# A mixer step fewer ahead of the experts, two mixer steps in pieces between expert tiles

## The chip, the cores and the metric

The kernel runs on one core of a Trainium2 chip. The metric is the time of one execution on the device in microseconds, as the median of several runs.

## The reference

The input x has 32 sequences of 256 tokens with 128 features, 8192 tokens in all. Two branches read its layer norm, and the output is x plus both.

```python
xn = layernorm(x)
# mixer
x_proj, z = split(xn @ W_in.T)                    # 256 and 256 features
x_conv = silu(causal_conv(x_proj, 4 taps) + conv_b)
B, C, dt_in = split(x_conv @ W_x.T)               # 16, 16, 256
dt = softplus(dt_in @ W_dt.T + b_dt)
alpha = sigmoid(0.1 * dt)
h = scan(clip(alpha, 0.01, 0.99), (1 - alpha) * sigmoid(mean(B)) * x_conv)
y = (h * sigmoid(mean(C)) + D * x_conv) * silu(z)
mixed = y @ W_out.T
# experts: 8 of them, 128 -> 256 -> 128, each token goes to its best two
hidden = silu(xt @ w1[e]) * (xt @ w3[e])
moe = sum over the two of softmax share * (hidden @ w2[e])
out = x + mixed + moe
```

## The kernel before

**Stages.** The opening normalises the rows, transposes them into `xnT` (16 groups of 512 tokens), computes the expert choices and a slot for every (token, expert) pair. POOL scatters each row to its two slots in DRAM (`moe_in`, line 600; 128 scatters of 128 rows). Meanwhile the mixer handles its 16 groups one after the other in steps. Then the experts work through `MOE_TILES` = 36 tiles: 31 of 512 rows of one expert, 4 whose halves belong to two experts, 1 of 256 rows. The tail finishes the mixer steps that are left, while POOL adds the experts' results, block by block, to the output (14 accumulating DMAs of 512 KB, line 628, in the order of `SUMS`).

**A mixer step.** On PE, step g is `project(g)` (L746, into PC), `gates(g)` (L703), `convolved(g)` (L755 and L759, the input of step g+1, into PA), `gated(g)` (L765, into PB), `spread(g)` (L717, the two gates of the step before, broadcast over the partitions) and `out(g)` (L731, the output product of the step before that). ACT computes softplus in parts (Abs L1133, Exp L1137, Ln L1139, between the table loads L1128 and L1157), the decay (`decay_th` L1110, `decay_al` L1118), the last tap (L1088) and the SiLUs (L1095, L1099, L1103). DVE has the other taps (L1492, three of them), `softplus(g)` (L1473), `turn(g)` (L1482), `add_out(g)` (L1502, adds an output to `xacc`) and `chain(g)`: seven operations counted in `s_ch` (L1386 to L1415), scans among them (L1404), and the product with the gated input (L1424).

`STEPS_A` = 12 steps (0 to 11) run ahead of the experts. Step 11 is the held one: ACT copies its gates from PSUM into `held_g` (L1148), so that PD becomes free for the experts, and DVE does the chain of step 11 between tiles 0, 1 and 2. Step 12 is begun among the tiles: PE's `spread(12)` behind tile 1, the decay on ACT at tiles 3 and 4, DVE's `early_chain` at tiles 4 to 11, and `project(12)` just before the last down product. Steps 12 to 15 are finished in the tail.

**Row scatters.** `follow` (line 575) holds each of the 128 scatters back. From the 39th on, nine go into each mixer step, released by `pace(g, at)`:

```python
def pace(g, at):
    at_chain = {1: 1, 3: 4, 5: 5, 6: 6, 7: 7}
    ...
elif i >= 39:
    pace((i - 39) // 9 + 1, (i - 39) % 9)
```

**An expert tile.** PE: `up(t)` (L861, L862, L865: twelve products of 512 columns in a split of high and low parts, to PA and PB), `transp(t + 1)` (L842, to PD), `down(t - 1)` (L899, sixteen products, to the other half of PD). ACT: rounds the next weights (`round_w`, L1173), `gate(t)` (SiLU of PA, L1202), rounds the next rows (`round_x`, L1196). DVE: low part of weights (L1635) and rows (L1622), `glu` (L1629), the shares and destinations (L1662 to L1681), `scale_y` (L1690, scales a tile's result into one of `OUTS` = 8 buffers). POOL scatters the result of each tile in four scatters (L614), paced by PE's progress. SP loads weights and rows. All engines work in the order in which their instructions are written. On PE tiles 2 to 27 are a hardware loop over pairs (`pe.Fori`), on ACT tiles 11 to 28, on DVE loops of eight tiles; the others are written out.

**Stores.** Blocks of 1024 tokens whose mixer part is complete go to the output by SP (`store_base`, L449 and L451; `STORED` = 6 blocks): four ahead of the experts, the fifth behind the loads of tile 3, the sixth (L491) behind the last expert load. The sums of blocks 0 to 5 are added in the output itself; block 6 is summed in `xacc`, block 7 on PE from rows that SP loads (L497).

## Time and profile before

| | |
|---|---|
| median of 3 runs | 474.4 us (473.97 to 475.49) |
| span of the profiled execution | 553.9 us |
| PE busy | 459.8 us (83%) |
| DVE busy | 394.6 us (71%) |
| POOL busy | 312.4 us (56%) |
| ACT busy | 288.3 us (52%) |
| granted TensorE clock, mean | 0.945 |

The profile is of one execution with the profiler on, whose own time is its span; the runs are made without it. Busy shares are of the span. The profile's lines speak of idle time before an instruction and of what released it; "remote" and "another core or an unknown queue" mean that a semaphore moved at a time for which no instruction's record accounts. A "x4" in a timeline merges four instructions; a matmul of 512 columns in full precision appears as two.

### The profile page before, as it was taken

The page shows a single profiled execution, that of the slowest core. Times are in us where ns is not written, and L with a number is a line of the kernel's source. Part 1 is how long each engine was busy: PE and PEld are TensorE (multiplying, and loading weights), DVE is VectorE, ACT ScalarE, POOL GpSimd, SP SyncE. Part 2 cuts the span into 40 slices and gives each one's busy share as a digit, 9 for nine tenths or more (in the row PEclk, how much of TensorE's full clock was granted, in tenths as well). Part 3 has the DMA queues.
Part 4 walks back from the last instruction along what each step waited for, and adds up shares of the span by engine and source line. Part 5 has one row for each costly group of instructions (what it writes and reads, how often), then busy time and mean ns, then how long its engine had stood idle before and what let it go on. Part 6 is the DMA issues. An engine that isn't in the chain of part 4 may idle for free.

```text
span 553.9 us, 8718 instructions
## 1 busy us (share of the span) xinstructions
PE 459.8 (83%) x2440; PEld 324.4 (59%) x2440; DVE 394.6 (71%) x836; ACT 288.3 (52%) x406; POOL 312.4 (56%) x344
## 2 busy tenths in 40 slices
PE   0987646999999999879979869696987798979876
PEld 0884222445544455448867658585876688745455
DVE  5997551989999999878856675454635465549987
ACT  3772126878888888785533333232423232466880
POOL 4657763767767675711666656565665655663300
PEclk9999777899999999999989999797989898899999
DMA  9921114112121212235556544453543453209992
GB/s 249 283 84 52 54 64 163 50 36 83 49 77 44 82 44 72 78 98 152 164 172 179 168 134 143 120 147 122 156 135 113 126 162 107 71 2 189 243 210 80
DMA packets 48076, 65.91 MB, mean 119 GB/s; under 512 B 8424, under 2 KB 30223, under 8 KB 48048
## 3 DMA queue, kind: packets, MB, share of 16 engines
q1 hardware_dynamic: 36240, 39.56, 25.5%
q0 software_dynamic: 10656, 24.47, 16.1%
q10 hardware_dynamic: 1152, 1.57, 0.9%
q8 instruction: 10, 0.16, 0.1%
q14 instruction: 18, 0.15, 0.1%
HBM read 42.09 MB, written 33.83 MB: 137 GB/s over the span
## 4 chain that ended last, share of the span: by engine, by line
PE 31%; DVE 22%; another core or an unknown queue 18%; issue 16%; ACT 8%; SPq 2%; DMA 1%; DVEq 1%; ACTq 0%
PE PC L746 5%; PE PB L731 4%; PE PD L899 4%; DVE hbuf L1404 3%; PE PA L759 2%; DVE hbuf L1415 2%; DVE gbuf L1289 2%; PE PA L865 2%; PE PA L861 1%; DVE gbuf L1386 1%; DVE xnT L1690 1%; PE PA L862 1%; DVE y L1424 1%; DVE al L1389 1%
## 5 line engine op out<-in xcount | busy, mean ns | idle before, releaser
L614 POOL DMA_INDIRECT moe_out<-xnT,dst_u x142 | 143.1, 1008 | 114.7 <-DVE xnT L1690 51.2
L600 POOL DMA_INDIRECT moe_in<-xn,slot_u x128 | 137.7, 1076 | 65.6 <-issue 41.1
L1202 ACT ACTIVATE xn<-PA 128x1024 f32<-128x1024 f32 (+1 forms) x36 | 36.5, 1015 | 95.1 <-PE PA L865 52.0
L1629 DVE TENSOR_TENSOR xn<-xn,PB 128x1024 f32<-128x1024 f32 (+1 forms) x36 | 43.3, 1204 | 43.1 <-remote 19.0
L899 PE MATMUL PD<-xnT,xn 128*128 128x128 f32 x536 | 68.1, 281 | 6.1 <-DVE xnT L1690 5.7
L899 PEld LDWEIGHTS PD<-xnT,xn 128*128 128x128 f32 x536 | 64.2, 196 | 8.5 <-issue 4.9
L746 PE MATMUL PC<-xc,Wc 128*128 128x512 f32 x128 | 59.9, 612 | 2.8 <-ACT xc L1099 2.8
L759 PE MATMUL PA<-xnT,Wtap 128*128 (+4 forms) x128 | 59.1, 604 | 0.4 <-issue 0.4
L1690 DVE TENSOR_TENSOR xnT<-PD,slot_p 128x512 f32<-128x512 f32 (+1 forms) x36 | 24.5, 681 | 39.6 <-remote 35.1
L861 PE MATMUL PA<-xhi,whi 128*128 128x512 f32 x62 | 29.4, 474 | 26.6 <-ACT xhi L1196 16.7
L1196 ACT ACTIVATE xhi<-PD 128x512 fp32r<-128x512 f32 (+1 forms) x36 | 21.2, 589 | 49.7 <-remote 32.6
L759 PEld LDWEIGHTS PA<-xnT,Wtap 128*128 128x128 f32 x128 | 24.9, 195 | 32.8 <-issue 32.8
L746 PEld LDWEIGHTS PC<-xc,Wc 128*128 128x128 f32 x128 | 24.0, 197 | 28.1 <-issue 24.8
L765 PE MATMUL PB<-xnT,WinT 128*128 (+1 forms) x64 | 31.7, 620 | 7.9 <-ACT nbdt L1009 7.7
L1492 DVE SCALAR_TENSOR_TENSOR acc<-PA,cw,acc 128x510 f32<-128x510 f32 (+2 forms) x48 | 35.6, 741 | 3.4 <-ACT acc L1088 2.4
L1404 DVE TENSOR_TENSOR_SCAN hbuf<-al,gbuf 128x512 f32<-128x512 f32 x30 | 35.0, 1208 | 0.1
L1133 ACT ACTIVATE ebuf<-PC,bdt 128x512 f32<-128x512 f32 x32 | 20.3, 684 | 24.4 <-PE PC L746 15.3
L1622 DVE TENSOR_TENSOR xlo<-PD,xhi 128x512 fp32r<-128x512 f32 (+1 forms) x36 | 24.4, 678 | 11.7 <-ACT xhi L1196 10.3
L731 PE MATMUL PB<-WoT,y 128*128 128x128 f32 x192 | 25.9, 292 | 5.8 <-DVE y L1424 4.9
L861 PEld LDWEIGHTS PA<-xhi,whi 128*128 128x128 f32 x62 | 12.8, 207 | 30.3 <-issue 28.7
L1110 ACT ACTIVATE th<-ebuf,bdt 128x512 f32<-128x512 f32 x32 | 21.3, 714 | 14.7 <-issue 12.8
L731 PEld LDWEIGHTS PB<-WoT,y 128*128 128x128 f32 x192 | 23.9, 202 | 8.5 <-DVE y L1424 6.6
(244 smaller groups left out, 963.2 us busy)
## 6 DMA issues: line engine op xcount, KB each, us to landing
xnT<-moe_w SPq DMA_DIRECT2D x36, 256.0 KB
xn<-moe_in SPq DMA_DIRECT2D x31, 266.0 KB
out_dram<-moe_out POOLq DMA_DIRECT2D x12, 512.0 KB, 11.8
xnT<-moe_w SPq DMA_DIRECT2D x36, 128.0 KB
out_dram<-xacc SPq DMA_DIRECT2D x7, 512.0 KB, 10.0
moe_out<-xnT,dst_u POOLq DMA_INDIRECT x142
moe_in<-zrow SPq DMA_DIRECT2D x8, 266.0 KB
moe_w<-in_L_ffn_w_dram SPq DMA_DIRECT2D x2, 1024.0 KB
```

The source lines that it names most:

```text
L600: gp.indirect_dma_start(xs_dram, bass.IndirectOffsetOnAxis(ap=slot_u[:, k, j:j + 1], axis=0), xn_row[:, j, :], None).then_inc(s_scat, 16)
L614: gp.indirect_dma_start(yt_dram, bass.IndirectOffsetOnAxis(ap=dst_u[:, t, j:j + 1], axis=0), yo[t % OUTS][:, j, :], None, bounds_check=PAI ...
L731: last = pe.matmul(PB[:, at + j * D:at + (j + 1) * D], y[:, k, j * P:(j + 1) * P], WoT[:, k, :], start=(k == 0), stop=(k == 1))
L746: last = pe.matmul(PC[:, c_ * GROUP:(c_ + 1) * GROUP], Wc[:, k, c_ * P:(c_ + 1) * P], xc[:, slot, k, :], start=(k == 0), stop=(k == 1))
L759: last = pe.matmul(both[:, :, j:SEQ], Wtap[:, TAPS - 1 - j, :], src[:, :, 0:SEQ - j], start=(j == 0), stop=(j == TAPS - 1))
L765: last = pe.matmul(PB[:, c_ * GROUP:(c_ + 1) * GROUP], WinT[:, INNER + c_ * P:INNER + (c_ + 1) * P], source(g), start=True, stop=True)
L861: pe.matmul(o, whi[:, b, at], xhi[:, b, :], start=True, stop=False)
L899: last = pe.matmul(PD[:, 512 + j * D:512 + (j + 1) * D], hid[b][:, k * SLOTS + j * P:k * SLOTS + (j + 1) * P], (w2x[t - FULL] if mixed and ...
L1202: act.activation(halves(sil, t), halves(PA[:, :], t), ACT.Silu).then_inc(s_sil, 1)
L1404: last = ve.tensor_tensor_scan(hbuf[:, c_, :], al[:, c_, :], gbuf[:, c_, :], 0.0, ALU.mult, ALU.add)
L1492: ve.scalar_tensor_tensor(a_v, p_v[:, :, 0:SEQ - j], cw[:, 1, TAPS - 1 - j:TAPS - j], a_v, ALU.mult, ALU.add).then_inc(s_taps if j == TAPS ...
L1629: ve.tensor_tensor(halves(hid[b], t), halves(sil, t), halves(PB[:, :], t), ALU.mult).then_inc(s_hid, 1)
```

## The change

Eleven steps (0 to 10) run ahead, step 10 is the held one. Steps 11 and 12 (`INNER_STEPS` = 2) are done in twelve pieces each, at the tiles in `INNER_AT` for step 11 and 15 tiles (`CYCLE`) later for step 12; step 13 (`STEPS_B`) gets its first five pieces at tiles 31 to 35. On PE the pieces are 1 `spread`, 2 gates, 3 `out`, 4 and 5 the halves of `project`, 8 and 9 the halves of `convolved`, 10 `gated`. All of them use PC in place of PA, PB and PD. ACT copies the spread gates to `held_g` at piece 1 (`hold_among`) for each of these steps, and has the table loads with exponential and logarithm in piece 6. DVE has `chain` cut into eight (`chain_among`) with `turn`, `add_out`, `softplus` and the taps. All loops over tiles on PE, ACT and DVE are written out. In the tail, steps 13 to 15 are left. From the 39th scatter on, ten go into a step; the tenth waits for the step's softplus. SP's fifth `store_base` moves behind its loop over tiles.

```diff
-STEPS_A = 12
+STEPS_A = 11
+INNER_STEPS = 2
+STEPS_B = STEPS_A + INNER_STEPS
+CYCLE = 30 // INNER_STEPS
+INNER_AT = (1, 2, 4, 5, 7, 8, 10, 11, 13, 14, 16, 17)
...
-STORED = STEPS_A // 2
+STORED = 6
...
+        def pieces(t):
+            found = [(STEPS_A + n, at + 1) for n in range(INNER_STEPS) for at in range(len(INNER_AT))
+                     if n * CYCLE + INNER_AT[at] == t]
+            last = t - INNER_STEPS * CYCLE
+            return found + [(STEPS_B, last)] if last >= 1 else found
...
-            sp.wait_ge(s_xp, 12)
-            sp.wait_ge(s_z, 12)
+            sp.wait_ge(s_xp, 11)
+            sp.wait_ge(s_z, 11)
...
-            store_base(STORED - 2)
-
             with sp.Fori(0, (FULL - 4) // 2) as i:
...
+            store_base(STORED - 2)
...
-                else:
-                    gp.wait_ge(s_y2, g)
+                elif at == 8:
+                    gp.wait_ge(s_y2, g)
+                else:
+                    gp.wait_ge(s_dt, g + 1)
...
-                    pace((i - 39) // 9 + 1, (i - 39) % 9)
+                    pace((i - 39) // 10 + 1, (i - 39) % 10)
...
+            def mixer_piece(g, at):
+                if at == 1:
+                    spread(g)
+                elif at == 2:
+                    gates_among(g)
+                elif at == 3:
+                    out(g, g % SLOT3, True)
+                elif at == 4:
+                    project_among(g, 1)
+                elif at == 5:
+                    project_among(g, 0)
+                elif at == 8 and g < STEPS_B:
+                    convolved_among(g, 0)
+                elif at == 9 and g < STEPS_B:
+                    convolved_among(g, 1)
+                elif at == 10 and g < STEPS_B:
+                    gated_among(g)
...
-            spread(STEPS_A)
-            with pe.Fori(0, (FULL - 4) // 2) as i:
-                up(i * 2 + 2, 0, False)
-                transp(i * 2 + 3, i + 1, 1, False)
-                down(i * 2 + 1, i, 1, False)
-                up(i * 2 + 3, 1, False)
-                transp(i * 2 + 4, i + 2, 0, False)
-                down(i * 2 + 2, i + 1, 0, False)
-            for t in range(2 + (FULL - 4) // 2 * 2, MOE_TILES):
+            for piece in pieces(1):
+                mixer_piece(*piece)
+            for t in range(2, MOE_TILES):
...
                 down(t - 1, (t - 1) // 2, (t - 1) % 2, False)
-            project(STEPS_A, STEPS_A % SLOT3, True)
+                for piece in pieces(t):
+                    mixer_piece(*piece)
...
+            def mixer_piece(g, at):
+                if at == 1:
+                    hold_among(g)
+                    decay_th(g)
+                elif at == 2:
+                    decay_al(g)
+                elif at == 4:
+                    row_tanh(g)
+                elif at == 5:
+                    abs_among(g)
+                elif at == 6 and g < STEPS_B:
+                    act.preload_act_table_set("natural_log_exp_and_others")
+                    logs_among(g)
+                    act.preload_act_table_set("silu_and_others")
...
-            turns = (FULL - 1 - opening) // 2
-            with act.Fori(0, turns) as i:
-                tile_step(i * 2 + opening, i + opening // 2, 1, True)
-                tile_step(i * 2 + (opening + 1), i + (opening + 1) // 2, 0, True)
-            for t in range(opening + 2 * turns, MOE_TILES):
+            for t in range(3, MOE_TILES):
                 tile_step(t, t // 2, t % 2, t + 1 < MOE_TILES)
+                for piece in pieces(t):
+                    mixer_piece(*piece)
...
+            for t in range(3, MOE_TILES):
                 static_step_v(t)
+                for piece in pieces(t):
+                    mixer_piece(*piece)
...
+            g = STEPS_B
+            chain_among(g, 3)
+            chain_among(g, 4)
+            softplus(g)
+            for n in (5, 6, 7):
+                chain_among(g, n)
+            for g in range(STEPS_B, GROUPS - 1):
```

## Rows read from the trace of the kernel before

**Rows 1.** Page: the span.

```profile
span 553.9 us, 8718 instructions
```

**Rows 2.** Page, part 4: shares of the chain that ended last, by engine.

```profile
PE 31%; DVE 22%; another core or an unknown queue 18%; issue 16%; ACT 8%; SPq 2%; DMA 1%; DVEq 1%; ACTq 0%
```

**Rows 3.** Busy time by stage: opening, mixer steps, expert tiles, tail.

```profile
core 0: us, PE busy (x) PEld busy (x) DVE busy (x) ACT busy (x) POOL busy (x), PEclk, DMA share, GB/s
0.00:96.30 96.30, 60.98 (x300) 41.89 (x301) 62.05 (x276) 42.09 (x87) 56.67 (x98) 0.90 0.45 137
96.30:238.20 141.90, 133.98 (x621) 71.35 (x621) 130.22 (x169) 113.03 (x140) 99.96 (x90) 0.98 0.20 63
238.20:482.80 244.60, 205.97 (x1220) 175.19 (x1219) 147.22 (x320) 91.39 (x129) 134.22 (x133) 0.93 0.47 138
482.80:553.90 71.10, 58.85 (x304) 35.94 (x302) 55.13 (x72) 41.79 (x53) 21.55 (x23) 0.98 0.67 142
```

**Rows 4.** The same view: tiles 3 to 28, tiles 29 to 34, tiles 21 and 22.

```profile
261.90:432.60 170.70, 143.28 (x834) 121.72 (x833) 102.15 (x221) 57.17 (x81) 103.17 (x103) 0.94 0.50 146
432.60:477.40 44.80, 37.06 (x242) 33.95 (x241) 23.85 (x56) 15.61 (x23) 25.96 (x27) 0.89 0.44 125
383.90:393.90 10.00, 10.00 (x65) 8.86 (x64) 5.87 (x14) 3.42 (x6) 5.92 (x6) 1.00 0.34 101
```

**Rows 5.** Waits in the expert tiles: us in total, times, longest.

```profile
ACT xhi L1196 <- remote: 32.6, 8, 6.1
```

**Rows 6.** Timeline of ACT in the opening.

```profile
59.20 0.60 ACT L1006 ACTIVATE Wc<-PB 128x512 f32<-128x512 f32 x1 [7.36 <-issue]
...
69.00 1.02 ACT L1082 ACTIVATE sz<-PB 128x1024 f32<-128x1024 f32 x1 [7.83 <-remote]
```

**Rows 7.** Timeline of PE: first projections of two mixer steps, eight steps apart.

```profile
111.33 0.59 PE L746 MATMUL PC<-xc,Wc 128*128 128x512 f32 x1
...
222.54 0.59 PE L746 MATMUL PC<-xc,Wc 128*128 128x512 f32 x1
```

**Rows 8.** Timeline of PE: one mixer step.

```profile
195.37 3.60 PE L746 MATMUL PC<-xc,Wc 128*128 128x512 f32 x8
198.81 1.88 PE L765 MATMUL PB<-xnT,WinT 128*128 x4
200.62 0.64 PE L703 MATMUL PD<-xc,WgS 128*32 128x128 f32 x16
...
202.15 3.58 PE L759 MATMUL PA<-xnT,Wtap 128*128 x8
205.57 1.05 PE L717 MATMUL PD<-ident,tg 128*128 128x128 f32 x8
207.09 2.05 PE L731 MATMUL PB<-WoT,y 128*128 128x128 f32 x16 [0.47 <-DVE y L1424]
```

**Rows 9.** Timeline of POOL: two of the last row scatters.

```profile
232.50 0.96 POOL L600 DMA_INDIRECT moe_in<-xn,slot_u  x1 [0.30 <-issue]
...
235.47 1.62 POOL L600 DMA_INDIRECT moe_in<-xn,slot_u  x1 [0.30 <-issue]
```

**Rows 10.** Timeline of ACT ahead of the first expert tile.

```profile
242.15 1.28 ACT L1128 ACT_TABLE_LOAD   x1
243.45 1.27 ACT L1133 ACTIVATE ebuf<-PC,bdt 128x512 f32<-128x512 f32 x2
244.75 1.06 ACT L1137 ACTIVATE ebuf<-ebuf 128x1024 f32<-128x1024 f32 x1
```

**Rows 11.** Timeline of PE in the tail: projections of steps 14 and 15.

```profile
514.29 3.70 PE L746 MATMUL PC<-xc,Wc 128*128 128x512 f32 x8 [1.35 <-ACT xc L1099]
...
527.03 2.41 PE L746 MATMUL PC<-xc,Wc 128*128 128x512 f32 x5 [1.41 <-ACT xc L1099]
```

**Rows 12.** Timeline of POOL: the last scatter of expert rows.

```profile
493.90 0.98 POOL L614 DMA_INDIRECT moe_out<-xnT,dst_u  x1 [0.30 <-issue]
```

**Rows 13.** Busy time while the sums run.

```profile
496.80:539.60 42.80, 38.54 (x192) 22.57 (x190) 39.31 (x50) 33.29 (x42) 12.70 (x14) 0.96 1.01 206
```

More of the change, by code:

```diff
@@ L832, in _, with gates_among @@
             pe.sem_inc(s_out, 1)
-            mixer(pe, mix, 0, STEPS_A)
+            mixer(pe, mix, 0, STEPS_A - 1)
+            mixer(pe, mix, STEPS_A - 1, STEPS_A)
+            def gates_among(g):
+                slot = g % SLOT3
+                pe.wait_ge(s_xc, g + 1)
+                pe.wait_ge(s_hold, holds(g))
+                for k in range(HALVES):
+                    for j in range(STRIPS):
+                        last = pe.matmul(PC[j * STRIP:(j + 1) * STRIP, GROUP:GROUP + P], WgS[:, k, :],
+                                         xc[:, slot, k, j * P:(j + 1) * P], start=(k == 0), stop=(k == 1))
+                last.then_inc(s_g, 1)
@@ new lines, in project_among @@
+            def project_among(g, c_):
+                slot = g % SLOT3
+                if c_ == 1:
+                    pe.wait_ge(s_lt, g + 1)
+                else:
+                    pe.wait_ge(s_add, g)
+                for k in range(HALVES):
+                    last = pe.matmul(PC[:, c_ * GROUP:(c_ + 1) * GROUP], Wc[:, k, c_ * P:(c_ + 1) * P],
+                                     xc[:, slot, k, :], start=(k == 0), stop=(k == 1))
+                if c_ == 0:
+                    last.then_inc(s_u, 1)
@@ new lines, in convolved_among @@
+            def convolved_among(g, part):
+                both = PC[:, 0:GROUP].rearrange("p (s l) -> p s l", s=SPG)
+                src = source(g).rearrange("p (s l) -> p s l", s=SPG)
+                if part == 0:
+                    pe.wait_ge(s_dt, g + 1)
+                    pe.matmul(PC[:, GROUP:2 * GROUP], WinT[:, P:2 * P], source(g), start=True, stop=True).then_inc(s_xr, 1)
+                for j in range(2 * part, 2 * part + 2):
+                    last = pe.matmul(both[:, :, j:SEQ], Wtap[:, TAPS - 1 - j, :], src[:, :, 0:SEQ - j],
+                                     start=(j == 0), stop=(j == TAPS - 1))
+                if part == 1:
+                    last.then_inc(s_xp, 1)
@@ new lines, in gated_among @@
+            def gated_among(g):
+                pe.wait_ge(s_c0, g + 2)
+                pe.wait_ge(s_taps, g + 2)
+                for c_ in range(HALVES):
+                    last = pe.matmul(PC[:, c_ * GROUP:(c_ + 1) * GROUP],
+                                     WinT[:, INNER + c_ * P:INNER + (c_ + 1) * P], source(g), start=True, stop=True)
+                last.then_inc(s_z, 1)
+            def mixer_piece(g, at):
[15 more added lines that the diff above has]
+                    gated_among(g)
@@ L934, in _ @@
             pe.wait_ge(s_hid, MOE_TILES)
-            gates(STEPS_A, STEPS_A % SLOT3, True)
-            for g in range(STEPS_A, GROUPS - 1):
+            for g in range(STEPS_B, GROUPS - 1):
                 pe.wait_ge(s_taps, g + 1)
@@ L1212, in tile_step, with hold_among, abs_among @@
                     round_x(t + 1, 1 - b)
+            def hold_among(g):
+                act.wait_ge(s_gb, g)
+                act.wait_ge(s_ch, (g - 2) * CHAIN + C_USED)
+                act.activation(held_g[:, :, :], PC[:, :].rearrange("p (n l) -> p n l", n=2), ACT.Copy).then_inc(s_hold, 1)
+            def abs_among(g):
+                act.wait_ge(s_u, g + 1)
+                act.wait_ge(s_th, g)
+                for c_ in range(HALVES):
+                    last = act.activation(ebuf[:, c_, :], PC[:, c_ * GROUP:(c_ + 1) * GROUP], ACT.Abs,
+                                          bias=bdt[:, c_:c_ + 1])
+                last.then_inc(s_abs, 1)
@@ L1231, in _ @@
             round_x(2, 0)
+            for piece in pieces(1):
+                mixer_piece(*piece)
             round_w(3, 1, 1, False)
```

182 lines of the change are left out of this document (108 added, 74 removed).

## The prediction

> **What bounds the kernel now.** The page's first line gives a span of 553.9 us [rows 1]; the unprofiled runs have a median of 474.4 us, 79.5 us less. The chain of waits shows what kind of time differs: 18% of the span (about 100 us) is put down to no engine [rows 2]. The view by stage cuts the span into four [rows 3]: the opening 96.3 us, eleven mixer steps and a bit 141.9 us (PE busy 134.0), the expert tiles 244.6 us, the tail 71.1 us. In the expert tiles, two neighbours can run at 5.0 us each with PE busy all the time, yet 32 tiles take 170.7 + 44.8 = 215.5 us, 6.73 each, 55.5 us over 32 x 5.0 [rows 4]. The excess sits in single holes: ACT waits eight times, up to 6.1 us, for a transpose whose record had long ended [rows 5]. ACT shows the same holes in the opening, 7.36 and 7.83 us [rows 6]. I read them as mostly the profile's own cost, since the runs are 79.5 us shorter and nothing else has such holes. The sum is therefore a difference, made in the profile's durations and added to 474.4; by itself it would put the next span near 551.
>
> How much of the 55.5 is real decides the sign. If the opening owes only its two longest ACT waits [rows 6], 15.2 of the 79.5 us, the other 64 are more than all holes of the tiles: no slack, 5.0 us per tile. If it owes twice that and the tail 4, the tiles owe 45 and keep 10 us in which PE really waits. Call this slack s, between 0 and 10.
>
> **One step fewer ahead.** From the projection of one step to that of the eighth after it: 222.54 - 111.33 = 111.2, so 13.9 us a step [rows 7]. Removed: **-13.9**. Everything that waits on the step count moves with it: SP's first weight loads wait for eleven convolutions instead of twelve, the held gates for step 10.
>
> **Row scatters.** 128 scatters, 39 before the paced ones; 89 at nine a step end in step 10, at ten a step in step 9. The last one runs at 235.47 [rows 9], just ahead of the first tile, and would stand in the same place relative to the shorter front. POOL needs 0.96 + 0.30 = 1.26 us for one [rows 9], so ten take 12.6 of 13.9: it fits with 1.3 us left. No row shows ten in a step. Its price lies between 0 and, if each of the eight added ones held a step up whole, 8 x 1.26 = 10 us; a gain has no source, as their number is the same. I take **0**, because nine already run beside 13.9 us steps with 2.6 us idle.
>
> **PE work put among the tiles.** One step on PE, start to start [rows 8]: projection 3.44 (195.37 to 198.81), gated input 1.81, gates and convolution 4.95 (200.62 to 205.57), spread 1.05, output 2.05 less the 0.1 in which it overlaps the next; together 13.2. Steps 11 and 12 go in whole, step 13 without convolution (4.95 less 0.64 for the gates) and gated input: 3 x 13.2 - 4.3 - 1.8 = 33.5. Spread and projection of step 12 stood there already: 1.05 + 3.44. Net **+29.0** us of PE among 36 tiles. Where PE is busy without a hole all of it is on the path; the slack covers s.
>
> **DVE and ACT among the tiles.** DVE works 102.15 / 26 = 3.9 us in a tile [rows 4]; a piece adds 0.7 to 2.3. With 5.0 us and PE's own piece beside it, it fits but for the tiles of two experts, where it comes level. ACT is the tight one: piece 6 puts table load, exponential, logarithm and table load in one run, 1.28 + 1.06 + 1.06 + 1.28 = 4.7 us [rows 10], in a tile with no PE piece to stretch it (tiles 8 and 23). With the tile's own 57.17 / 26 = 2.2 us [rows 4] ACT needs 6.9 where PE needs 5.0. PE can go on for about 0.4 us of that: 1.5 us lost, twice. **+3**. From below 0 (a late gate covered), from above 10 (every piece of ACT and DVE a hole of half a microsecond, some twenty of them).
>
> The row shows the next activation 0.02 us behind the table load, 243.45 against 242.15 + 1.28 [rows 10]. The Trainium skill, "ScalarE: Activation LUTs", section "What ACT_TABLE_LOAD costs", counts a drain of 1.38 us with each switch; four switches would then cost 5.5 us more, and the sum would end at 476.9 instead of 471.4. The trace shows no such drain, so I leave it out.
>
> **Other moves.** PE, ACT and DVE no longer loop over tiles. I cost that at 0: tiles 22 and 23 stand 5.0 us apart across a turn of PE's loop, and unlooped tiles (29 to 34, 44.8 / 6 = 7.5) have as many holes as looped ones (170.7 / 26 = 6.6) [rows 4]. ACT copies the spread gates to held_g, about 1.0 us a step, beside PE's next tile. SP moves one 512 KB store behind its loop and one ahead of the last scatter; nothing waits for either but the sums.
>
> **Tail.** One step fewer: projections of 14 and 15 stand 527.03 - 514.29 = 12.7 us apart [rows 11]. The first step is no faster: before, PE reaches project(13) behind two outputs; after, DVE reaches the taps of step 13 behind both scans, softplus and three chain pieces, by my count of its rows at the same point, 16 us behind the last up product. **-12.6**, if the DMAs allow it (a rival below). Bounds: -6 by that rival, -15 if both outputs' 3.8 us come off too.
>
> **Sum.** -13.9 + 29.0 - s + 3 - 12.6 = +5.5 - s. For s I take 8.5, nearer to 10 than to 0: POOL issues four scatters a tile at 0.98 + 0.30 us [rows 12], 5.1 us, so that tiles can't average 5.0, and 36 x 0.1 = 4 us of slack are there by this alone; and the wait of 7.36 us in the opening [rows 6] is a hole of the same kind as the others, which speaks for the larger share there. So -3.0: **471.4 us**. Break-even is s = 5.5. With s from 10 to 4 this case runs from 469.9 to 475.9; below s = 4 it is the first rival.
>
> **Rivals.** *PE has no slack* (slower). Place: PE's in-order queue in the tiles. s = 0 and 6 us of stalls instead of 3 (a piece waits for DVE's scan or ACT's copy, and the next up product queues behind it): -13.9 + 29.0 + 6 - 12.6 = +8.5, **482.9**. It decides as soon as s falls under what the pieces stall plus 2.5. For it: 10.0 of 10.0 us busy in tiles 21 and 22 [rows 4]. Against: POOL's 5.1 us a tile.
>
> *The holes are real* (faster). If PE idles in the runs as in the profile, even by a third of the 55.5, pieces disappear in it: s = 20, **459.9**. For it: the chain of the profile. Against: the 79.5 us must come from somewhere, and the holes are the only place. The Trainium skill, "Runtime: NRT & Kernel Launch", section "Instruction fetch mechanics", says a taken branch can force a fetch before going on; 13 turns of PE's loop would then go away and the time would end in this rival's place. The trace speaks against it: unlooped tiles have the holes too.
>
> *The sums set the end* (no change or slower). The last scatter runs at 493.90 [rows 12], the end is 60.0 us later; a step less makes it 47.4. The sums hold the DMAs from 496.8 to 539.6, at a share of 1.01 and 206 GB/s [rows 13], and can't start before the last scatter: 45.7 us, less 2.5 for the 0.5 MB store that is now done earlier. That leaves 4 us for last rows, loads and stores, which now share the DMAs with the sums. If they queue behind them half of the tail's gain goes: -6 instead of -12.6, **478.0**.
>
> *It doesn't do what it says*: the tenth scatter waits for the softplus of its step, and if POOL then falls behind, the first rows are late; up to +10, inside the slower cases.
>
> **How the numbers follow.** A measurement tells 0.3%, 1.4 us, from no change. Forecast case 0.38 (faster 0.26, same 0.10, slower 0.02); holes real 0.19 (faster); no slack 0.30 (slower 0.28, same 0.02); sums 0.13 (faster 0.01, same 0.03, slower 0.09). Together faster 0.46, same 0.15, slower 0.39. The likeliest case's own range is 467 to 476. The whole range takes in the fast rival and the slow one with 2 us beyond: 458 to 485.
>
> **What would show it.** Right: first tile's transposes 14 us earlier; last transposes and last scatter about 20 us later relative to them, at unchanged or slightly higher cost per hole; tile pairs without pieces at 10.0 us, with pieces longer by exactly PE's piece; from last up product to the end 12 to 13 us less. Wrong: the tiles' stretch grows by clearly more than 28 or less than 12; ACT's piece 6 followed by a PE hole over 2 us; step length ahead of the experts over 14.5; DMA share at 1.0 up to the last store.

## The result, and the profile after

The changed kernel takes **496.0 us** (median of 4 runs, 495.7 to 497.3) beside 474.4 for the kernel before (474.0 to 475.5): ratio 1.047, interval 1.045 to 1.050 (the two medians alone give 1.046). It is slower by 21.6 us. Every ratio here leaves out single runs that took over 1.5% more than the fastest run of the same kernel. The prediction was 471.4 us, and its range (458 to 485) doesn't hold the result.

The page of the changed kernel, its first line, the line of PE, DVE, ACT and POOL, and the chain by engine, as [rows 1, 2]:

```profile
span 493.9 us, 8449 instructions
...
PE 434.3 (88%) x2440; PEld 310.6 (63%) x2440; DVE 394.2 (80%) x836; ACT 290.6 (59%) x409; POOL 316.3 (64%) x344
...
PE 47%; DVE 29%; issue 11%; ACT 6%; POOL 3%; DMA 2%; ACTq 0%; DVEq 0%; SPq 0%
```

The span is 2.1 us under the runs' median, and the 18% of "another core or an unknown queue" of [rows 2] is gone. So the trace of before that the prediction read and this trace don't show the same situation: its span was 79.5 us over its kernel's median. Which of the two is odd was settled by the experiments. They ran on four chips. On two of them the kernel before has medians of 473 to 475 us and shows no holes, on the other two it takes 545 to 561 us unprofiled as well; the two chips that were used in two series came out alike both times. The trace of [rows 1 to 13] looks like the second kind in its span and its holes; the two times of the result are of the first. I call them the 474 us chips and the 554 us chips. A profile of the kernel before on a 474 us chip (run i1) is therefore the one to hold against the profile after. Busy time by stage, cut at the transposes of the first and of the 36th expert tile; first the kernel before, on a 474 us chip:

```profile
core 0: us, PE busy (x) PEld busy (x) DVE busy (x) ACT busy (x) POOL busy (x), PEclk, DMA share, GB/s
0.00:217.60 217.60, 194.05 (x948) 113.32 (x948) 196.44 (x452) 162.54 (x236) 151.15 (x188) 0.98 0.35 105
217.60:393.40 175.80, 173.78 (x1145) 154.90 (x1146) 141.00 (x305) 84.06 (x117) 124.53 (x122) 1.00 0.63 184
393.40:472.10 78.70, 63.67 (x349) 40.35 (x347) 57.60 (x79) 42.65 (x54) 35.82 (x35) 0.94 0.62 137
238.10:363.00 124.90, 124.76 (x801) 110.66 (x800) 99.17 (x212) 56.50 (x78) 95.98 (x95) 1.00 0.65 192
```

then the changed kernel:

```profile
0.00:214.30 214.30, 179.79 (x887) 105.76 (x887) 184.84 (x437) 152.10 (x222) 150.49 (x188) 0.97 0.35 106
214.30:424.20 209.90, 204.84 (x1300) 173.40 (x1301) 157.42 (x329) 106.93 (x147) 137.84 (x129) 0.99 0.55 157
424.20:493.90 69.70, 49.63 (x256) 31.41 (x254) 51.97 (x70) 31.62 (x40) 28.01 (x28) 0.89 0.69 148
```

Front 3.3 us shorter, 35 tiles 34.1 longer, tail 9.0 shorter: -3.3 + 34.1 - 9.0 = +21.8, the difference of the spans (493.9 - 472.1). In the tiles PE was busy 173.78 of 175.80 us before (124.76 of 124.90 in the middle ones) and is busy 204.84 of 209.90 after: 31.1 us more work and 3.0 us more idle time. Some 1.5 us of that work is the first tile, which holds no piece: PE is busy for 5.55 us in it, at a granted clock of 0.58, where it was for 4.04 us at 1.00.

**The front, after.** POOL's last two row scatters, SP's loads of the first rows, PE's first transposes:

```profile
207.63 0.96 POOL L617 DMA_INDIRECT moe_in<-xn,slot_u  x1 [0.30 <-issue]
208.90 0.96 POOL L617 DMA_INDIRECT moe_in<-xn,slot_u  x1 [0.30 <-issue]
```

```profile
211.38 0.85 SPq L482 DMA_DIRECT2D xn<-moe_in  x2
```

```profile
214.28 1.09 PE L923 MATMUL PD<-ident,xn 128*128 128x128 f32 x4 [11.60 <-DMA xn<-moe_in]
```

PE has finished its eleventh step at 202.7 us, where it finished the twelfth at 217.2 before, and waits 11.6 us for rows; they can be loaded only behind the 128th scatter. From 205.3 to 214.2 us PE and ACT do nothing. In the kernel before, the last scatter starts at 210.48 and PE comes to the tiles at 217.62, 0.44 us of wait behind DVE:

```profile
210.48 0.96 POOL L600 DMA_INDIRECT moe_in<-xn,slot_u  x1 [0.30 <-issue]
```

```profile
217.62 0.66 PE L842 MATMUL PD<-ident,xn 128*128 128x128 f32 x4 [0.44 <-DVE lgt L1482]
```

**The tail, after.** POOL's last expert scatter and first sum, and VectorE's last addition (the span ends at 493.94):

```profile
442.98 0.98 POOL L631 DMA_INDIRECT moe_out<-xnT,dst_u  x1 [0.30 <-issue]
445.88 1.27 POOL L645 DMA_DIRECT2D xacc<-moe_out  x1 [1.92 <-issue]
```

```profile
485.65 0.42 DVE L1915 TENSOR_TENSOR xacc<-PB,xacc 128x256 f32<-128x256 f32 x1 [0.47 <-PE PB L1059]
```

The same of the kernel before on a 474 us chip (its span ends at 472.10):

```profile
421.01 0.98 POOL L614 DMA_INDIRECT moe_out<-xnT,dst_u  x1 [0.30 <-issue]
423.90 1.50 POOL L628 DMA_DIRECT2D xacc<-moe_out  x1 [1.91 <-issue]
```

```profile
463.74 0.42 DVE L1773 TENSOR_TENSOR xacc<-PB,xacc 128x256 f32<-128x256 f32 x1 [0.47 <-PE PB L983]
```

The end stands 48.1 us behind the first sum after, 48.2 before, and 7.9 us behind the last addition in both. In the kernel before, POOL issues the 142 scatters of expert rows from 231.72 to 421.01 us with a single pause of over 0.4 us (0.56 us): they are a chain as unbroken as PE's, only later. In the changed kernel the same chain has 26 such pauses, 25.7 us in all, in which it waits for the slower tiles. In the trace that the prediction read, the last addition stood 2.3 us before the end, and the tail looked as if VectorE and PE set it.

### The profile page after: what moved, and what is told of

Read it like the earlier page. It is cut to its first block, busy times and chain, and to the rows that moved or that the text cites. A ratio compares the mean times of both kernels' runs of the same rounds, so it can differ in the third digit from the quotient of the medians.

```text
span 493.9 us, 8449 instructions
## 1 busy us (share of the span) xinstructions
PE 434.3 (88%) x2440; PEld 310.6 (63%) x2440; DVE 394.2 (80%) x836; ACT 290.6 (59%) x409; POOL 316.3 (64%) x344
## 4 chain that ended last, share of the span: by engine, by line
PE 47%; DVE 29%; issue 11%; ACT 6%; POOL 3%; DMA 2%; ACTq 0%; DVEq 0%; SPq 0%
PE PD L980 10%; DVE hbuf L1529 4%; PE PB L753 4%; DVE hbuf L1540 3%; POOL moe_in L617 3%; PE PD L923 3%; PE PA L946 3%; PE PB L942 2%; PE PB L943 2%; PE PB L946 2%; PE PA L942 2%; DVE gbuf L1511 2%; DVE gbuf L1414 2%; PE PA L943 2%; DVE acc L1618 2%
## 5 line engine op out<-in xcount | busy, mean ns | idle before, releaser
L631 POOL DMA_INDIRECT moe_out<-xnT,dst_u x142 | 153.6, 1082 | 80.5 <-issue 33.8
L617 POOL DMA_INDIRECT moe_in<-xn,slot_u x128 | 131.6, 1028 | 44.6 <-issue 40.6
L766 PE MATMUL PC<-xc,Wc 128*128 128x512 f32 x104 | 49.8, 624 | 5.8 <-ACT xc L1175 5.8
L779 PE MATMUL PA<-xnT,Wtap 128*128 (+4 forms) x112 | 51.6, 604 | 0.0
L1761 DVE TENSOR_TENSOR wlo<-xnT,whi 128x512 fp32r<-128x512 f32 x36 | 24.7, 685 | 15.3 <-ACT whi L1249 15.1
L1618 DVE SCALAR_TENSOR_TENSOR acc<-PA,cw,acc 128x510 f32<-128x510 f32 (+2 forms) x42 | 31.0, 739 | 1.2 <-ACT acc L1164 0.9
L923 PE MATMUL PD<-ident,xn 128*128 128x128 f32 x142 | 21.8, 276 | 11.6 <-DMA xn<-moe_in 11.6
L1186 ACT ACTIVATE th<-ebuf,bdt 128x512 f32<-128x512 f32 x32 | 21.3, 713 | 13.2 <-DVE ebuf L1598 13.2
L923 PEld LDWEIGHTS PD<-ident,xn 128*128 128x128 f32 x142 | 17.7, 142 | 15.9 <-issue 11.8
L785 PE MATMUL PB<-xnT,WinT 128*128 128x512 f32 (+1 forms) x56 | 26.5, 596 | 1.2 <-ACT bdt L1086 1.0
L1598 DVE SCALAR_TENSOR_TENSOR ebuf<-PC,nbdt,ebuf 128x512 f32<-128x512 f32 x32 | 22.4, 740 | 3.2 <-ACT ebuf L1215 2.0
```

Of the source, the lines that this page charges most:

```text
L617: gp.indirect_dma_start(xs_dram, bass.IndirectOffsetOnAxis(ap=slot_u[:, k, j:j + 1], axis=0), xn_row[:, j, :], None).then_inc(s_scat, 16)
L631: gp.indirect_dma_start(yt_dram, bass.IndirectOffsetOnAxis(ap=dst_u[:, t, j:j + 1], axis=0), yo[t % OUTS][:, j, :], None, bounds_check=PAI ...
L766: last = pe.matmul(PC[:, c_ * GROUP:(c_ + 1) * GROUP], Wc[:, k, c_ * P:(c_ + 1) * P], xc[:, slot, k, :], start=(k == 0), stop=(k == 1))
L779: last = pe.matmul(both[:, :, j:SEQ], Wtap[:, TAPS - 1 - j, :], src[:, :, 0:SEQ - j], start=(j == 0), stop=(j == TAPS - 1))
L785: last = pe.matmul(PB[:, c_ * GROUP:(c_ + 1) * GROUP], WinT[:, INNER + c_ * P:INNER + (c_ + 1) * P], source(g), start=True, stop=True)
L923: last = pe.transpose(PD[:, j * P:(j + 1) * P], xs[b][:, j, 0:D], ident[:, :])
```

## Experiments on the 554 us chips

The first three series ran on chips on which the kernel before takes 551 to 560 us.

**The kernel before again**, twice for a profile (e0, f0): 550.9 and 560.7 us, beside medians of 554.2 and 560.2 for other runs of it.

> The kernel before, unchanged, profiled once more. The changed kernel's profile has a span (493.9) close to its runs (496.0), the one of before did not (553.9 against 474.4). If the holes were an accident of that one profiled execution, this span is near 472 and the expert tiles stand 5.2 to 5.4 us apart; if they belong to the looped kernel under the profiler, it is again near 554 and the holes are back.

> The kernel before, unchanged, for a profile beside the other three on whatever chip this is. Where its runs take 474, I expect a span near 472, no holes, expert tiles 5.2 to 5.4 us apart and an opening some 20 us shorter than in the trace of 553.9. Where they take 554, the same picture as in that trace.

The 35 tiles take 224.0 us in e0 and 232.6 in f0, against 232.7 in the prediction's trace, and the unprofiled time is just as long as the profiled one. The holes are no cost of the profiler, though the prediction had read them so. They go with the chip, or with something around it that no run separates from it. Busy time in the tiles of the kernel before, in f0:

```profile
248.60:481.10 232.50, 195.53 (x1144) 166.32 (x1145) 139.73 (x305) 83.04 (x117) 132.18 (x130) 0.93 0.49 141
```

**The changed kernel again** (f1): 549.3 us, ratio 0.983 (0.974 to 0.993).

> The changed kernel, unchanged, beside the kernel before on one chip. Where the kernel before takes 474: 496 again, 4.7% slower. Where it takes 554 (a chip on which engines stall while POOL's scatters run): theory A, ten scatters a step bring the stalls up, 570 to 590; rival, the holes among the tiles swallow the pieces, 535 to 550.

The change that costs 4.7% on a 474 us chip gains 1.7% here, in the rival's range. The same view of it:

```profile
242.00:472.30 230.30, 212.28 (x1301) 174.46 (x1302) 157.40 (x331) 107.93 (x150) 134.65 (x129) 0.99 0.49 143
```

PE is busy for 16.8 us more in 2.2 us less time: most of the pieces lie in the holes. The pieces need 31.1 us on a 474 us chip, and the clock accounts for the difference of 14.3. The tiles of the kernel before keep PE busy for 195.53 us here, at a granted clock of 0.93 (173.78 at 1.00 on a 474 us chip), those of the changed kernel for 212.28 at 0.99 (204.84 at 0.99). That the filled holes are what keeps the clock up is my reading of these four rows; it was not tried alone.

**Ten row scatters in a step of the kernel before** (e1, f2):

```diff
-                else:
-                    gp.wait_ge(s_y2, g)
+                elif at == 8:
+                    gp.wait_ge(s_y2, g)
+                else:
+                    gp.wait_ge(s_dt, g + 1)
...
-                    pace((i - 39) // 9 + 1, (i - 39) % 9)
+                    pace((i - 39) // 10 + 1, (i - 39) % 10)
```

> The kernel before with ten row scatters a step instead of nine, the tenth behind the softplus; nothing else. Theory A (POOL's scatters are a chain of their own; twelve steps leave it room): no change, 473 to 476, last scatter 5 to 12 us earlier than with nine. Rival (a tenth scatter slows each step): 8 steps longer by up to 1.3 us each, 478 to 484.

> The kernel before with ten scatters a step. On a chip without the stalls: no change (within 2 us of the kernel before), because POOL only finishes earlier. With the stalls: 2.7% slower as measured once already (567 against 554).

Ratios 1.027 (1.014 to 1.041) and 1.023 (1.013 to 1.034): slower here, by 12 to 15 us, which neither the first expectation nor its rival had, since both were made for a 474 us chip.

**Row scatters not paced at all in the changed kernel** (e2; from the 40th on `pace` is left out):

> The changed kernel with the scatters from the 39th on not paced at all. Theory A (the front of the changed kernel waits some 9 us for the last scatter, which paced scatters reach at 208.9 us; unpaced ones end near 200): first tile's transposes at 205 to 207 instead of 214.3, time 487 to 490. Rival (the pace is what keeps the scatters off the steps): steps longer, first tile no earlier, time 495 or more.

621.7 us, ratio 1.130. Busy time of two stretches while the scatters run one behind another:

```profile
100.00:120.00 20.00, 16.83 (x86) 8.43 (x84) 14.35 (x20) 11.25 (x14) 15.43 (x16) 1.00 0.16 52
140.00:160.00 20.00, 2.56 (x11) 2.17 (x12) 3.50 (x6) 0.21 (x1) 15.42 (x16) 0.50 0.16 55
```

POOL works as before, and in the second stretch the others nearly stand still, at a DMA share of 0.16. The last scatter starts at 213.8 us, 21 earlier than in f1, and still PE reaches the first tile only at 323.0 (242.0 in f1): the loss is in the steps and not in the scatters. I can't say what the engines wait for. It goes with the kind of chip: on the 474 us chips POOL issues its scatters without a pause too, as i1 to i3 below show, and the steps keep their 13.4 us.

**Twelve steps ahead, one among the tiles, nine scatters** (e3, f3), and **eleven ahead, one among the tiles, ten scatters** (g1):

```diff
-STEPS_A = 11
-INNER_STEPS = 2
+STEPS_A = 12        (11 in g1)
+INNER_STEPS = 1
...
-                    pace((i - 39) // 10 + 1, (i - 39) % 10)
+                    pace((i - 39) // 9 + 1, (i - 39) % 9)        (not in g1)
```

> The changed kernel with twelve steps ahead and one among the tiles (STEPS_A = 12, INNER_STEPS = 1) and nine scatters a step: only the tail's step is moved. Theory A (11 us of the loss are the scatters at the end of a shorter front, the rest is that PE has no slack among the tiles): front as before, one step of PE work less among the tiles, 478 to 484. Rival (the loss is all in the pieces): 485 to 490. If tiles had slack for one step: 464 to 472.

> Twelve steps ahead, one among the tiles, nine scatters a step. On a chip without the stalls, theory A (some 10 us of the 21.6 are the wait for scatters ahead of the first tile, the rest is PE work among tiles without slack): 478 to 484. Rival (the pieces cost it all): 485 to 490. With the stalls: 547 as measured already.

> Eleven steps ahead, one among the tiles, ten scatters a step (STEPS_A = 11, INNER_STEPS = 1): only the front's step is moved, the tail keeps four. On a chip where the kernel before takes 474: the front gives 14 back less 11 of waiting for scatters, one step and five pieces (15.8 us of PE beyond what stood there) go among the tiles, so 480 to 488 by the theory that the tiles have little slack; under 474 if the loss were in the tail. Where it takes 555: 548 to 560, near the changed kernel, if stalls swallow pieces.

Ratios 0.9925 (0.987 to 0.998), 0.984 (0.972 to 0.996) and 1.015 (1.008 to 1.022); the first two are the same kernel in two series. On such a chip a step moved from the tail to the tiles gains, and one moved there from the front doesn't.

## Experiments on the 474 us chips

**A profile of the kernel before** (i1, 473.9 us):

> The kernel before, unchanged, for a profile on a chip on which it takes 474 us. Both theories: no stretch in which all engines stand still among the tiles, steps ahead 13.4 us apart, first expert tile's transposes at 217.8 as in the kernel with twelve steps ahead and one among the tiles. Theory 1 (no slack): its 35 tiles take 180 us (5.0 each and five longer ones), and the time from the 36th tile's transposes to the end is 74 to 76. Theory 2 (the tiles had slack, and the tail is what grew): tiles of 190 and a tail of 64. Where it takes 554: the profile shows holes again.

No holes; tiles 175.8 us, tail 78.7. Theory 1's numbers were off by 4 (tiles) and 3 (tail), theory 2's by 14 and 15. The rows stand above.

**The same two variants of the split** (h2, h3):

> Twelve steps ahead, one among the tiles (13 in all before the tail's last), nine row scatters a step: against the kernel before, one step leaves the tail and goes into the tiles. If the tiles have no slack and the tail is held by its DMAs, 474 + 14.5 - 3 = 486 (ratio 1.024) on a chip where the kernel before takes 474; if the tail gives all of its 12.6 us, 476. Where the kernel before takes 554: 0.984 to 0.993, as in two earlier runs.

> Eleven steps ahead with ten row scatters each, one step among the tiles, the tail as before: one step leaves the front. If the scatters' own time bounds the front (10 x 1.27 us of 13.4 a step) the front gives 3 of its 13.9 us and the tiles take 14.5: 474 + 11.5 = 485 (ratio 1.024) where the kernel before takes 474; if the front gives all of it, 475. Where the kernel before takes 554: 1.015, as in an earlier run.

487.6 us (ratio 1.029, 1.027 to 1.032) and 489.6 us (1.034, 1.032 to 1.037). Busy time in the tiles and tail, of h2, then of h3:

```profile
217.80:412.50 194.70, 190.22 (x1238) 164.39 (x1239) 146.11 (x314) 96.28 (x133) 133.24 (x127) 1.00 0.58 168
412.50:485.80 73.30, 49.82 (x256) 31.54 (x254) 51.94 (x70) 31.64 (x40) 30.85 (x30) 0.87 0.66 143
```

```profile
214.00:409.20 195.20, 191.26 (x1239) 165.93 (x1240) 144.75 (x312) 95.48 (x132) 133.58 (x127) 0.99 0.58 168
409.20:487.30 78.10, 62.96 (x318) 38.61 (x316) 65.75 (x87) 42.80 (x54) 30.47 (x30) 0.93 0.62 134
```

The first moved step costs 18.9 to 19.4 us among the tiles (194.7 and 195.2 against 175.8), the second 14.7 (209.9 against 195.2). The first brings five pieces of the next step with it: of its 18.9 us in h2, 16.4 are work of PE (190.22 against 173.78) and 2.5 idle time. A step fewer ahead gives 3.3 to 3.8 us (217.6 or 217.8 to 214.0 or 214.3). A step fewer in the tail gives 5.4 (78.7 to 73.3, i1 to h2) or 8.4 (78.1 to 69.7, h3 to the changed kernel). The expectations had 14.5 for the tiles in both, 4.4 to 4.9 us too little, so both kernels came out slower than expected. Neither a shorter front nor a shorter tail pays what a step among the tiles costs; the split of the kernel before is the best of the four on such a chip.

The tail of h3 shows a second path. Its last expert scatter stands 21.3 us behind the 36th tile's transposes, 6.3 less than in i1, yet its tail is only 0.6 us shorter. Its last addition ends 75.9 us behind the same transposes (70.8 in i1) and 2.2 us before the end: with four steps left the mixer sets the end there. The changed kernel has one step less, its last addition comes 61.9 us behind the 36th tile's transposes instead of 75.9, and the sums set the end again.

**Thin pieces** (h1): the pieces' matmuls stream 8 columns, which leaves out most of the mixer's values of three steps. (The convolution's stream 4, and `spread` is as it was.)

```diff
...
-                    last = pe.matmul(PC[:, c_ * GROUP:(c_ + 1) * GROUP], Wc[:, k, c_ * P:(c_ + 1) * P],
-                                     xc[:, slot, k, :], start=(k == 0), stop=(k == 1))
+                    last = pe.matmul(PC[:, c_ * GROUP:c_ * GROUP + 8], Wc[:, k, c_ * P:(c_ + 1) * P],
+                                     xc[:, slot, k, 0:8], start=(k == 0), stop=(k == 1))
...
```

> The changed kernel in which the matmuls of the pieces that follow expert tiles stream 8 columns where they streamed 128 to 512 (the same number of matmuls, waits and signals; the mixer's values of steps 11 to 13 are left out thereby). Theory 1 (TensorE sets the tiles' pace, no slack): on a chip where the kernel before takes 474 us it takes some 20 us less than the changed kernel's 496, about 475, and tiles with a piece of TensorE start 5.3 us apart where they started 6.7. Theory 2 (the pieces on ScalarE and VectorE set it): within 5 us of 496. On a chip where the kernel before takes 554 us, theory 3 (there each tile waits for something that is no engine's work, and the pieces lie under these waits): at most 5 us less than the changed kernel (549 in an earlier run, 0.983 of the kernel before), against 20 less, 0.947, by theory 1.

480.1 us, 15.9 under the changed kernel; the tiles take 195.6 us, 14.3 less, and PE is busy in them for 190.15, 14.7 less. Most tiles with a piece of PE stand 5.4 us apart where they stood 6.7. Time and PE's work fall together: PE sets the tiles' pace, and ACT's and DVE's pieces, all still there, don't, but for the two tiles behind ACT's piece 6 (below). That it fell by 16 and not by 20 is due to how little a narrow matmul saves; the two groups of PE in the tiles of h1:

```profile
L754 PE MATMUL PC<-WoT,y 128*128 128x8 f32 x48 | 5.6, 251 | 0.0
...
L875 PE MATMUL PC<-xc,Wc 128*128 128x8 f32 x16 | 2.0, 236 | 0.0
```

The first number is the busy time of the group in us, in which overlapping matmuls count once, the second the mean of one in ns. In the changed kernel the same two groups are 5.8 us (275 ns each, 128 columns) and 7.5 us (593 ns, 512 columns): 8 columns save nothing against 128, and three quarters against 512.

**Ten scatters in the kernel before** (i2) and **eleven in the changed kernel** (i3; `// 11` and `% 11`, the eleventh waits for nothing):

> The kernel before with ten row scatters in each step ahead in place of nine, nothing else. Theory 1 (GpSimd's own time bounds the front only where eleven steps are to cover it): the last of twelve steps ends after the scatters either way, ratio 0.998 to 1.003. Theory 2 (a tenth scatter disturbs each step): steps of 13.4 grow to 14 or more, 12 x 0.6 = 7 us, ratio 1.015. Where the kernel before takes 554: 1.023 to 1.027 as in two earlier runs.

> The changed kernel with eleven row scatters paced into a step in place of ten (the eleventh waits for nothing). 11 x 1.27 = 14.0 us is more than a step's 13.4, so GpSimd is never idle from the first step on: 89 scatters from 84.6 on end at 198 instead of 208.9. Theory 1 (the scatters' own time holds the first tile back): its transposes start 5.4 us behind the last scatter, at 203 to 206 in place of 214.3, and the time is 8 to 11 us under the changed kernel's 496, 485 to 488. Theory 2 (unpaced scatters slow the other engines' steps): steps grow, the time is 496 or more. Where the kernel before takes 554: theory 2's outcome.

i2: 473.7 us, ratio 0.9989 (0.997 to 1.000): on this kind of chip the tenth scatter costs nothing. i3: 496.6 us, as the changed kernel; theory 1's 485 to 488 is a miss, and theory 2's time is right for the wrong reason, since the steps keep their 13.4 us. The scatters' times say why. In the kernel before, nine a step:

```profile
88.19 0.96 POOL L600 DMA_INDIRECT moe_in<-xn,slot_u  x1 [0.30 <-issue]
...
180.89 1.13 POOL L600 DMA_INDIRECT moe_in<-xn,slot_u  x1 [0.30 <-issue]
182.33 0.96 POOL L600 DMA_INDIRECT moe_in<-xn,slot_u  x1 [0.31 <-issue]
```

These are the 40th, 109th and 110th: 70 scatters in 94.1 us, 1.344 us each and not 1.26, because some of them take 1.13 to 1.30 us instead of 0.96, and with no more than 0.30 us between them. PE takes 94.1 us for seven steps (90.25 to 184.39). POOL already issues ten in a step without a pause, with a pacing of nine, ten or eleven alike, since it starts behind its schedule. The chain is in fact unbroken from its first scatter on, which starts at 36.7 to 36.9 us in these kernels: up to the 112th no pause is over 0.32 us. Ahead of the 114th POOL pauses for 3.1 to 3.7 us, for which the view names no releaser; in i1 it also waits 1.0 us ahead of the 113th. The last scatter starts at 210.5, 209.9, 208.9 and 210.1 us in i1, i2, the changed kernel and i3.

Some three of the ten in a step are long, 27 of the 89 from the 40th on in i1 (one of them takes 1.46 us), and each of these runs beside one of VectorE's operations whose data all lie in SBUF (L1386 and L1389, L1404, L1415 and L1424), such as the first row beside the second:

```profile
176.77 1.30 POOL L600 DMA_INDIRECT moe_in<-xn,slot_u  x1 [0.30 <-issue]
```

```profile
176.08 2.33 DVE L1404 TENSOR_TENSOR_SCAN hbuf<-al,gbuf 128x512 f32<-128x512 f32 x2
```

The Trainium skill, "SBUF — State Buffer", section "SBUF: two separate sides", says that GpSimd can't write its descriptors while some of VectorE's operations hold the port that both share. By that rule each long scatter would be a short wait for this port. The trace agrees, though not simply because the two overlap: 42 of the 62 short ones overlap such an operation at some time too. What tells the two kinds apart is one moment, which I took from the trace itself, 0.15 us behind the scatter's start. Such an operation is running then in all 27 long ones and in none of the 62 short ones of i1, and in i2 in 26 of 26 and none of 63. The added length grows with what is left of that operation: 0.17 us where it ends 0.30 us behind the scatter's start, 0.31 where it ends 0.44 behind it, 0.33 for 0.52. Still, no run took such an operation away, so the cause is argued and not shown.

**Ten fills of an unused buffer between the last scatters** (two ahead of each from the 117th to the 121st), in the changed kernel (j1) and in the kernel before (j2):

```diff
+                        if j * TOP_K + k in (116, 117, 118, 119, 120):
+                            gp.wait_ge(s_fill, 16 * EXPERTS)
+                            for n in range(2):
+                                gp.wait_ge(s_zrow, 1 + 2 * (j * TOP_K + k - 116) + n)
+                                gp.memset(zrow[:, :, :], 0.0).then_inc(s_zrow, 1)
```

> The changed kernel with ten fills of a 128 x 532 buffer (0.56 us each in the profile of the kernel before, 0.6 to 0.7 with their waits) put on GpSimd between the 117th and the 121st row scatter; nobody reads the buffer any more. Theory 1 (GpSimd's chain of 128 scatters sets when the tiles begin): the last scatter starts 6 to 7 us later, at 215 to 216, the first tile's transposes at 220 to 221, and the time is the changed kernel's 496 and 6 to 7: 502 to 503 (ratio 1.060). Theory 2 (the steps or a wait set it, and the scatters have room): 496 to 498. Where the kernel before takes 554: no statement, the changed kernel is 0.983 there.

> The same ten fills in the kernel before. Theory 1: its last scatter starts at 210.5, and 5.4 us behind it is 215.9, while its twelve steps let the tiles begin at 217.6, so it has 1.7 us of room: the tiles begin 4.3 to 5.3 us later and the time is 479 (ratio 1.009 to 1.011). Theory 2 (twelve steps cover the scatters with a whole step's room): ratio 1.000 to 1.002.

j1: 503.1 us, ratio 1.059 (1.055 to 1.063), 7 us over the changed kernel, as theory 1 said (6.5 in the front, and 0.6 in a first tile of 6.85 us instead of 6.28). The last scatter and PE's first transposes in j1:

```profile
215.46 0.96 POOL L622 DMA_INDIRECT moe_in<-xn,slot_u  x1 [0.30 <-issue]
```

```profile
220.81 1.09 PE L928 MATMUL PD<-ident,xn 128*128 128x128 f32 x4 [17.40 <-DMA xn<-moe_in]
```

Both are 6.5 us later than in the changed kernel: in its front POOL's chain of 128 scatters has no room at all. j2: 480.5 us, ratio 1.013 (1.009 to 1.016), 6.0 us against the 4.3 to 5.3 expected. Its front grows by 3.8 us, so the kernel before has under 2 us of room; and its tiles grow by 1.8 (399.0 less 221.4 against 175.8), all of it in the first one (7.08 us instead of 5.17), though not one instruction was added to them. The granted clock shows it. The first tiles in j2, behind 5.2 us in which PE stood still, and the same stretch of i1:

```profile
221.40:241.90 20.50, 19.01 (x97) 15.97 (x98) 15.18 (x32) 10.36 (x15) 3.80 (x4) 0.82 0.48 134
```

```profile
217.60:238.10 20.50, 18.62 (x105) 14.95 (x106) 18.16 (x38) 12.10 (x17) 5.16 (x5) 1.00 0.50 141
```

A share of 0.82 of the 2.4 GHz, an average of both levels, against 1.00; in the same 20.5 us PE finished 97 instructions instead of 105.

**Fewer sums** (i4): six of the fourteen sums in the changed kernel's tail are cut to an eighth (64 of 512 KB; the expectation calls it a quarter), so most rows of the second choice are left out of the stored blocks.

```diff
+                if k < STORED and c:
+                    gp.dma_start(dst[:, 0:1], yt_b[:, k, c, 0:1], accum_op=ALU.add).then_inc(s_got[k], 16)
+                    continue
```

> The changed kernel with six of its fourteen sums in the tail cut to a quarter of their 512 KB (the second choice's rows of the six stored blocks are left out for three quarters of the tokens in them). Theory 1 (the DMAs set the end, 7.8 us behind VectorE's last add): the last store follows the last add by 2 to 3 us, 5 us less in all: 491. Theory 2 (the mixer's last steps set the end): under 1 us less.

490.2 us, 5.8 under the changed kernel. The size of the six, from the issues of DMAs in this run, and the last addition, which is where it was; the span ends at 488.32, 2.3 us behind it instead of 7.9:

```profile
out_dram<-moe_out POOLq DMA_DIRECT2D x6, 64.0 KB, 9.5
```

```profile
485.62 0.42 DVE L1918 TENSOR_TENSOR xacc<-PB,xacc 128x256 f32<-128x256 f32 x1 [0.47 <-PE PB L1062]
```

In the changed kernel the DMAs set the end, by 5.6 us. In the kernel before the end stands as far behind the last addition (7.9 us), but its sums were not cut.

## Why the prediction was wrong, point by point

**The reading of the holes was the root.** The step "I read them as mostly the profile's own cost" fails: on a 554 us chip the unprofiled runs take as long as the profile with the holes (550.9 to 560.7 us). From there the prediction mixed two situations, a trace of one kind of chip and a median of the other, and had to estimate every slack from the difference of 79.5 us.

**Slack s, taken as 8.5: it was 0.** On a 474 us chip PE is busy 124.76 of 124.90 us in the middle tiles, and 99% of all of them. The argument that POOL's 5.1 us a tile would make PE wait fails too: the tiles stand 5.0 us apart and POOL falls behind them instead, its last expert scatter starting 27.6 us after the 36th tile's transposes. That the chosen 8.5 alone gave the forecast its sign is shown by the sum: with s = 0 the sum was +5.5.

**One step fewer ahead, -13.9: it gave -3.3.** The step itself is right (13.4 us on this chip, and PE has finished its steps 14.5 us earlier, at 202.7 instead of 217.2), but "the last one would stand in the same place relative to the shorter front" fails. The scatters are a chain of their own, which ends at 209 to 210.5 us whatever the number of steps; j1 shows that it has no room. The term "row scatters: 0" rested on 1.26 us apiece and on "1.3 us left" in a step; the scatters take 1.344, ten of them a whole step, and the bounds looked at what a scatter does to a step and not at what 128 of them need (172 to 174 us from the first to the last). The rival of the late tenth scatter gave up to +10 for this; its place was right, its mechanism (the wait for softplus) was not: in the changed kernel no scatter up to the 113th waits over 0.32 us for anything.

**PE pieces, +29.0: +31.1 measured.** Some 1.5 us of it are the first tile at a lower clock (0.58), which follows PE's wait for the rows; j2 shows the same without any piece. The rest, 29.6, is close to the forecast. **Stalls, +3: 3.0** (5.06 us idle against 2.02). That the number is exact is partly luck, but the mechanism is the forecast's. PE's waits in the tiles after are for xhi and xlo:

```profile
PE PA L942 <- ACT xhi L1272: 2.1, 3, 0.8
PE PA L946 <- DVE xlo L1748: 1.5, 4, 0.6
PE PA L942 <- issue: 1.5, 2, 0.7
```

Two of the three waits for xhi stand right behind piece 6, in which ACT works from 269.27 to 276.68 us without a pause and so rounds the next rows (`xhi`) late:

```profile
269.27 0.60 ACT L1272 ACTIVATE xhi<-PD 128x512 fp32r<-128x512 f32 x1 [0.50 <-PE PD L923]
269.89 1.28 ACT L1320 ACT_TABLE_LOAD   x1
271.18 1.06 ACT L1305 ACTIVATE ebuf<-ebuf 128x1024 f32<-128x1024 f32 x1
272.28 1.06 ACT L1307 ACTIVATE ebuf<-ebuf 128x1024 f32<-128x1024 f32 x1
...
273.36 1.28 ACT L1322 ACT_TABLE_LOAD   x1
274.65 0.63 ACT L1249 ACTIVATE whi<-xnT 128x512 fp32r<-128x512 f32 x1
...
276.09 0.59 ACT L1272 ACTIVATE xhi<-PD 128x512 fp32r<-128x512 f32 x1
```

```profile
276.78 0.47 PE L942 MATMUL PA<-xhi,whi 128*128 128x512 f32 x1 [0.78 <-ACT xhi L1272]
...
278.23 0.73 PE L946 MATMUL PA<-xlo,whi 128*128 128x512 f32 x2 [0.30 <-DVE xlo L1748]
```

The same stands at 365.94 and 367.39 (0.77 and 0.31 us). So each piece 6 cost 1.1 us where 1.5 was forecast, 2.2 in all; the rest of the 3.0 are waits for xhi and xlo in early tiles, at 234 to 242 us.

**Unrolling, 0**: nothing in the traces speaks against it, but it was not tried alone.

**Tail, -12.6: it gave -9.0.** The rival "the sums set the end" has the mechanism. Both kernels end 48 us behind their first sum, which follows the last expert scatter. That scatter stands 27.6 us behind the 36th tile before and 18.8 after, because POOL catches up in the slower tiles: this gives 8.8 of the 9.0. It took the missing step as well: in h3 the mixer still has four steps left and sets the end, and the tail is only 0.6 us shorter than in i1, although POOL has caught up by 6.3. The mixer's own path got 8.9 us shorter than in i1 (last addition 70.8 us after the 36th tile's transposes before, 61.9 after), so without the sums the gain would still have been under the forecast's 12.6. The rival's 6 was nearer than the forecast's 12.6.

**The sum again**: -3.3 + 31.1 + 3.0 - 9.0 = +21.8. Against the predicted -3.0 that is 24.8 us, of which the front is 10.6, the slack 8.5, the tail 3.6 and the pieces 2.1. "PE has no slack" was the right rival for the tiles; at 482.9 it fell short because it kept the front's and the tail's gains whole. "The holes are real" is what happens on the 554 us chips, at a ratio of 0.983.

The rule of the Trainium skill, "ScalarE: Activation LUTs", section "What ACT_TABLE_LOAD costs", that I had set aside would have brought the sum to 476.9. The trace of the changed kernel doesn't agree with its drain of 1.38 us: all four loads among the tiles start 0.01 to 0.02 us behind the operation before them, and the next operation starts 0.01 to 0.02 us behind their end, as in the rows of piece 6 above.

**Open**: what the holes of the 554 us chips are, why the other engines stop there while unpaced scatters run (e2), and what POOL's pause ahead of the 114th scatter is. No version that I ran beats the kernel before on a 474 us chip; on a 554 us chip the changed kernel does, by 1.7%, and the split of e3 and f3, by 0.8 and 1.6%.

## What to carry to other kernels

If a profile's span is far from the median it should explain, first get a profile whose span agrees; no slack may be read from one that doesn't. When a stage is shortened, list every chain that must end before the next stage begins and sum each by itself, POOL's scatters too: a chain that ran under it with 2 us to spare takes over after 2 us. And ask of the end which engine's backlog starts it: here POOL's backlog and the mixer's last steps lay within 8 us of each other, so that by these rows a shorter mixer alone gains nothing and a shorter backlog alone no more than those 8 us.

## What the runs showed of the hardware that I had not expected

- A row scatter on POOL takes 0.96 us in most cases and 1.13 to 1.30 in others, in the same kernel and stage; the mean distance in the front is 1.344 us. The long ones are those behind whose start, by 0.15 us, VectorE is running an operation with all its data in SBUF: 27 of 27 in i1, and none of the 62 short ones.
- An f32 matmul of 128 x 8 takes 236 to 251 ns where 128 x 128 takes 275 and 128 x 512 takes 593. In PE's busy time it is 117 to 125 ns each (5.6 us / 48, 2.0 us / 16) against 121 and 469 (5.8 us / 48, 7.5 us / 16): fewer than 128 columns save nearly nothing.
- PE standing still for 5.2 us ahead of the tiles (j2) cost 1.9 us more in the first tile, at a granted clock of 0.50 in it. A longer stand cost no more: 11.6 us in the changed kernel cost 1.1 (0.58), 17.4 us in j1 cost 1.7 (0.52).
- The same change is 4.7% slower on one kind of chip and 1.7% faster on another.
